# A graph layer kernel: thinned neighbours marked by indirect writes of single elements instead of by matmuls, and PSUM banks shared out anew

## The chip, the cores and the metric

The kernel runs on one core of one Trainium2 chip. The metric is device microseconds of one execution, start to end. The times of the kernel before are 1410.16, 1417.88 and 1423.46 us; their median is 1417.88 us.

## The reference, cut to what matters

There are 16 batches of 1024 nodes with 64 channels. Layer 0 is a normalised adjacency product; layer 1 thins the neighbour lists, takes quantiles over the sorted neighbour values in every channel, and ends with two small matmuls.

```python
neigh = (adj_ > 0) & ~eye
rank = jnp.cumsum(ni, axis=-1) - ni
nb = ni.sum(-1)
skip = jnp.where(nb > T, (nb + K - 1) // K, 1)          # T = 10, K = 2
rem = neigh & (sk > 1) & (rank % sk == sk - 1) & mask[:, :, None]
rem = rem | jnp.swapaxes(rem, 1, 2)
adj_d = jnp.where(rem, 0.0, adj_)
vals = jnp.where(nd[..., None], x[:, None, :, :], jnp.inf)
s = jnp.sort(vals, axis=2)                               # quantiles 0.25, 0.5, 0.75
h = jax.nn.relu(out @ W1 + b1)
y = h @ W2 + b2
```

So a node with more than 10 neighbours marks at most two of them, the one at rank skip-1 and the one at rank 2*skip-1, and each marked edge goes in both directions.

## The kernel before, in words

Two batches make a group `g`; there are 8 groups. Each batch is first prepared, and then the two batches of a group are worked on together.

Preparation of a batch: SP loads the adjacency in 8 pieces of 512 KB into `AT` (ring of 3). DVE makes 0/1 neighbours from them (`neighbors`, L1163), PE multiplies them with the features (`messages`, L557) and takes running counts over them (`ranks_up`, L568) into one of the three banks of `psT`; ACT brings the counts into `VR` (`ranked`, L841). `VR` holds one row of codes, features, neighbour count and mask for every node, and there is a single `VR`: the counts of the next batch wait until its rows have been scattered. Then the thinned edges are found and taken out for the whole 1024 x 1024 matrix: POOL computes ranks from the neighbour counts (`thin`, L1439 to L1456, 11 small instructions for each half of a batch), ACT writes the distance of each code to them (`distance`, L848), DVE turns that into a matrix of removals `RM` (`removed`, L1169), PE adds code, removal and transposed removal (`codes`, L589 to L596) in `psT`, ACT brings the result back through a Relu (`coded`, L867) and counts what is left (`valid`, L873). POOL sorts nodes into classes by their number of neighbours (`classes`, from L1465; `nodes_ahead` on PE, `ahead` on ACT, `place` on DVE, whose result `RS` POOL turns into `IDX` at L1480), and scatters the eight tiles of rows to HBM in that order with one indirect DMA each (`scatter`, L1505).

Work on a group: SP reads the sorted rows back in 128-row pieces (`RR`, two buffers, L530), PE transposes them (`positions_up`, L604), ACT stores the positions (L884). DVE makes one-hot matrices from them (`one_hots`, L1194, L1205, L1209), PE gathers neighbour features with these (`gather`, L651, L660) into two banks `psG`, ACT brings them out (L952, L957). DVE sorts: L1276 and L1277 for the 128 nodes with most neighbours, the hub, L1227 and L1232 for the others. Weights are applied (L1243, L1252), and `overflow` ends the sorting of a group with the memset of `MARK` (L1370). Then come the two small matmuls and, on POOL, the indirect writes of the output (`put`, L1546).

The order of the work of all engines is one string, `ORDER`: each letter stands for one step of a strand, and each engine takes its own part of each step in that order. SP's loads are in the same order, so a load that waits holds up the loads behind it. POOL, too, takes its instructions strictly in order. In the string, U is a load of adjacency, D a count, s a code tile, c a count of what is left, S a scatter, L a load of sorted rows, d a half of a one-hot chunk, and B and r the steps of thinning.

## Time and profile before

| what | us |
|---|---|
| median of three runs | 1417.88 |
| span of the profiled execution, first to last instruction | 1381.6 |
| median less span, what lies around it | 36.3 |
| TensorE (PE) busy | 1209.3 |
| VectorE (DVE) busy | 1129.0 |
| ScalarE (ACT) busy | 958.9 |
| GpSimd (POOL) busy | 734.6 |

The profile is of one execution. A busy time is the time in which an engine has an instruction running; a matmul's end is modelled, so PE's figure is an upper reading. The wait rows give the idle time of an engine just before an instruction and the engine whose work ended it. A stretch between two times can be asked for its own busy times, and that tells more than a mean over the whole span.

### The profile page before, as it was taken

Reading aid. Unit: us, or ns where it says so; the run is one execution under the profiler, and the core shown is the slowest. Engines: PE = TensorE matmul, PEld = TensorE weight load, DVE = VectorE, ACT = ScalarE, POOL = GpSimd, SP = SyncE. Lnnn points to the kernel's source line nnn. Section 1 sums busy time; section 2 is a strip of 40 time slices with the busy share of each in tenths; the row PEclk is TensorE's granted clock in tenths of the full one; section 3 lists DMA queues with packets and bytes.
Section 4 is the critical chain, followed back from the end, with each engine's and each line's share of the span. In section 5 each row is a group of like instructions: output and inputs, shape, how many; then the busy total and the mean of one; then the engine's idle time right before and its main releaser. Section 6 shows DMA issues by size and latency. Waiting matters only on the chain.

```text
span 1381.6 us, 32444 instructions
## 1 busy us (share of the span) xinstructions
PE 1209.3 (88%) x12833; PEld 893.1 (65%) x12833; DVE 1129.0 (82%) x2060; ACT 958.9 (69%) x1755; POOL 734.6 (53%) x988
## 2 busy tenths in 40 slices
PE   4979999999899989999999989899898999688543
PEld 4757776867577676667767667667666676555221
DVE  3441379989899889999799989889897999888980
ACT  1787778887789678888678677777775888743311
POOL 0463434454558753876547665774477553721325
PEclk9988799999999999999799998999898999889655
DMA  4355543554245433535444433446134341331000
GB/s 136 130 161 181 157 140 107 196 176 145 83 156 159 141 113 102 159 115 171 126 135 138 135 109 112 140 136 208 52 116 125 103 141 46 133 87 36 8 9 15
DMA packets 119032, 167.08 MB, mean 121 GB/s; under 512 B 58816, under 2 KB 59472, under 8 KB 118864
## 3 DMA queue, kind: packets, MB, share of 16 engines
q1 hardware_dynamic: 103168, 117.72, 28.9%
q0 software_dynamic: 14336, 46.42, 8.8%
q8 instruction: 101, 1.65, 0.5%
q10 hardware_dynamic: 1360, 0.74, 0.2%
q14 instruction: 67, 0.55, 0.1%
HBM read 114.25 MB, written 50.59 MB: 119 GB/s over the span
## 4 chain that ended last, share of the span: by engine, by line
PE 42%; DVE 23%; POOL 14%; issue 8%; ACT 7%; DMA 4%; ACTq 1%; SPq 0%; POOLq 0%; DVEq 0%
PE psL L557 11%; PE psG L660 6%; PE psT L568 5%; POOL out L1546 5%; PE psG L651 4%; DVE HUB L1276 4%; DVE HUB L1277 4%; PE psM L706 3%; DVE OHB L1209 3%; PE psT L589 2%; POOL rows L1505 2%; PE psT L593 2%; PE psT L604 2%; PE psT L596 2%; DVE OHB L1194 2%
## 5 line engine op out<-in xcount | busy, mean ns | idle before, releaser
L557 PE MATMUL psL<-H0A,AT 128*128 128x65 f32 x2048 | 274.3, 296 | 12.4 <-issue 8.6
L557 PEld LDWEIGHTS psL<-H0A,AT 128*128 128x128 f32 x2048 | 266.3, 212 | 24.3 <-issue 21.1
L1505 POOL DMA_INDIRECT rows<-VR,IDX x128 | 171.1, 1336 | 87.3 <-ACT JUNK L873 48.0
L1276 DVE TENSOR_TENSOR HUB<-HUB 128x1472 f32<-128x1472 f32 (+6 forms) x224 | 184.8, 825 | 11.9 <-ACT HUB L984 9.0
L1277 DVE TENSOR_TENSOR HUB<-HUB 128x1472 f32<-128x1472 f32 (+6 forms) x224 | 188.6, 842 | 0.0
L568 PE MATMUL psT<-UM,NEIT 128*128 128x512 f16 (+3 forms) x1024 | 161.0, 306 | 21.0 <-ACT VR L841 11.3
L867 ACT ACTIVATE VR<-psT 128x512 f16<-128x512 f32 x256 | 149.1, 598 | 43.4 <-PE psT L596 33.3
L660 PE MATMUL psG<-OHB,HL 128*64 128x384 f16 (+5 forms) x2048 | 170.2, 316 | 9.3 <-DVE OHB L1209 4.2
L1546 POOL DMA_INDIRECT out<-FR x128 | 154.5, 1207 | 38.4 <-issue 36.3
L651 PE MATMUL psG<-OHB,HL 128*64 128x256 f16 (+1 forms) x2560 | 152.9, 279 | 6.9 <-ACT HUB L952 3.7
L848 ACT ACTIVATE RM<-VR,SK 128x1024 f16<-128x1024 f16 x128 | 138.0, 1151 | 20.2 <-POOL SK L1456 20.2
L651 PEld LDWEIGHTS psG<-OHB,HL 128*64 128x64 f16 x2560 | 137.0, 116 | 19.9 <-DVE OHB L1194 8.9
L568 PEld LDWEIGHTS psT<-UM,NEIT 128*128 128x128 f16 x1024 | 88.8, 101 | 88.6 <-ACT VR L841 15.0
L660 PEld LDWEIGHTS psG<-OHB,HL 128*64 128x64 f16 x2048 | 106.7, 111 | 58.9 <-issue 9.1
L984 ACT ACTIVATE HUB<-HUB 128x1472 f32<-128x1472 f32 (+5 forms) x168 | 90.7, 540 | 69.5 <-DVE HUB L1277 67.8
L873 ACT ACTIVATE JUNK<-VR 128x1024 int8<-128x1024 f16 x128 | 134.4, 1058 | 0.1
L1163 DVE TENSOR_SCALAR NEIT<-AT 128x1024 f16<-128x1024 f32 x128 | 90.8, 730 | 30.7 <-DMA AT<-in_adjt 30.7
L593 PEld LDWEIGHTS psT<-CH,RM 128*128 128x128 f16 x1024 | 83.7, 100 | 48.9 <-issue 4.6
L841 ACT ACTIVATE VR<-psT,CF 128x512 f16<-128x512 f32 x128 | 80.7, 697 | 46.9 <-PE psT L568 41.9
L589 PE MATMUL psT<-VR,CH 128*128 128x512 f16 x256 | 100.6, 393 | 10.3 <-DVE RM L1169 6.2
L593 PE MATMUL psT<-CH,RM 128*128 128x128 f16 x1024 | 107.3, 223 | 0.0
L841 ACT ACTIVATE VR<-psT,CB 128x512 f16<-128x512 f32 x128 | 79.7, 692 | 32.7 <-POOL CB L1426 16.7
(135 smaller groups left out, 2273.0 us busy)
## 6 DMA issues: line engine op xcount, KB each, us to landing
AT<-in_adjt SPq DMA_DIRECT2D x128, 512.0 KB, 4.7
RR<-rows SPq DMA_DIRECT2D x128, 288.0 KB
FR<-rows SPq DMA_DIRECT2D x16, 272.0 KB, 4.7
X<-in_x SPq DMA_DIRECT2D x16, 256.0 KB, 3.7
h<-VR SPq DMA_DIRECT2D x16, 256.0 KB
rows<-VR,IDX POOLq DMA_INDIRECT x128, 4.3
out<-FR POOLq DMA_INDIRECT x128
CH<-in_ch ACTq DMA_DIRECT2D x1, 192.0 KB, 4.5
```

Source lines behind the costliest of these rows:

```text
L557: m = e.matmul(ps["L"][:, 65 * t:65 * t + 65], AT[:, n % RING, kk, t * P:t * P + P], H0A[:, T * b + 2 * kp + kk, :], start=(kp == kk == t ...
L568: m = e.matmul(o[:, kk * P:COLS], half(t // 4)[:, at:at + P], UM[:, 0:COLS - kk * P], start=(kk == 0), stop=(kk == 3), skip_group_check=True)
L593: e.matmul(oj, RM[:, t, k * P:k * P + P], idh, start=False, stop=False, skip_group_check=True)
L651: m = e.matmul(bk[C * b:C * b + C, at:at + cols], HL[:, part, (2 * g + b) % 3, k, :], OHB[:, n % 2, b, k * cols:k * cols + cols], start=(k ...
L660: m = e.matmul(bk[C * b:C * b + C, 0:cols], HL[:, part, (2 * g + b) % 3, k, :], OHB[:, n % 2, b, kk * cols:kk * cols + cols], start=(k == ...
L841: e.activation(VR[:, t, COLS * ch:COLS * ch + COLS], t_bank(u), ACT.Identity, bias=bias).then_inc(t_empty, 1)
L848: e.activation(RM[:, t, :], VR[:, t, 0:N], ACT.Abs, bias=SK[:, 3, t:t + 1]).then_inc(a_abs, 1)
L867: e.activation(VR[:, k, 512 * ch:512 * ch + 512], t_bank(u), ACT.Relu).then_inc(t_empty, 1)
L1276: e.tensor_tensor(b0, a0, a1, ALU.max)
L1277: e.tensor_tensor(b1, a0, a1, ALU.min).then_inc(v_bat, 1)
L1505: e.indirect_dma_start(row_d[:, :], bass.IndirectOffsetOnAxis(ap=IDX[:, gb % 2, t:t + 1], axis=0), VR[:, t, :].bitcast(I32), None).then_in ...
L1546: e.indirect_dma_start(out_d, bass.IndirectOffsetOnAxis(ap=dst, axis=0), fr[:, rt, 0:2 * C].bitcast(F32), None).then_inc(d_out[g % 2], 16)
```

## The change

The matrix of removals is gone, with `codes`, `coded`, `distance` and `removed`. Codes stay in `VR` as they are, without Relu, and are scattered at once; the features, counts and flags go with them. What is thinned is taken out in HBM afterwards, for the hub's 128 rows alone, in five new steps for each batch: `hub` (SP loads the first 128 rows into `HB`), `thin` (8 small instructions on POOL), `find` (one `max_index` on DVE, which looks for the two marked ranks in each of the 128 rows), `rank` (`targets`: 9 small instructions on POOL, two indirect reads of 128 single elements from a table of ranks that SP writes in step `key`, and two indirect writes of 128 single fp16 elements into the nodes' own rows), and `take` (`take_out`: 5 small instructions and two indirect writes of 128 single elements into the rows of the other nodes). What is written is `GONE`, the value -1. The loads of sorted rows now wait for the last two writes (`d_gone`) instead of the scatters. The count of what is left runs on ACT over the loaded row `RR`, before its buffer is given back, instead of over `VR`. Batches have HBM tensors of their own for their rows, and a row is 2580 bytes in place of 2576. `psT` has two banks in place of three, and the gather three in place of two. Two broadcast matmuls are added to each `flags` step, which report if more than 128 nodes have over 10 neighbours; the branch for such inputs is rewritten too, and it is entered only if a flag is set. `ORDER` is a new string: it differs all through.

```diff
-TB = 3
+TB = 2
+GB = 3
...
-            add("T", "thin", g, b, hf)
-            for t in range(4 * hf, 4 * hf + 4):
-                add("B", "abs", g, b, t)
-                add("r", "rem", g, b, t)
...
-            for ch in range(2):
-                add("s", "sc", g, b, k, ch)
-            add("c", "cn", g, b, k)
             add("S", "sca", g, b, k)
+        for c, kind in (("H", "hub"), ("T", "thin"), ("i", "find"), ("B", "rank"), ("r", "take")):
+            add(c, kind, g, b)
...
+                add("c", "cn", g, b, rt)
...
-        ps = {k: ctx.enter_context(nc.psum_tensor("ps" + k, [P, 512], F32)) for k in ("L", "S", "G0", "G1", "M")}
+        ps = {k: ctx.enter_context(nc.psum_tensor("ps" + k, [P, 512], F32)) for k in ("L", "S", "G0", "G1", "G2", "M")}
...
+                elif kind == "key":
+                    g, b = a
+                    gb = 2 * g + b
+                    w.wait_ge(o_idx, gb + 1)
+                    e.dma_start(rank_d[gb].rearrange("(t p) o -> p (t o)", p=P), IDX[:, gb % 2, :], allow_slow_non_contiguous=True).then_inc(d_rt, 16)
+                elif kind == "hub":
+                    g, b = a
+                    gb = 2 * g + b
+                    for t in range(T):
+                        w.wait_ge(d_sca[t], 16 * (gb + 1))
+                    if gb:
+                        w.wait_ge(v_find, gb)
+                        w.wait_ge(o_adr, gb)
+                    e.dma_start(HB[:, :].bitcast(I32), rows(g, b)[0:P, :]).then_inc(d_hub, 16)
                 elif kind == "ldr":
                     g, b, rt = a
                     n = nth["ldr", g, b, rt]
-                    for t in range(T):
-                        w.wait_ge(d_sca[t], 16 * (2 * g + b + 1))
+                    w.wait_ge(d_gone[b], 32 * (g + 1))
                     if n >= 2:
                         w.wait_ge(t_full, t_use("turn", filled[n - 2][0], filled[n - 2][2]) + 1)
-                    n0 = (2 * g + b) * N + rt * P
-                    e.dma_start(RR[:, n % 2].bitcast(I32), row_d[n0:n0 + P, 0:R_X1 // 2]).then_inc(d_row[n % 2], 16)
+                        w.wait_ge(a_cn, n - 1)
+                    e.dma_start(RR[:, n % 2].bitcast(I32), rows(g, b)[rt * P:rt * P + P, 0:R_X1 // 2]).then_inc(d_row[n % 2], 16)
...
-            def codes(g, b, k, ch):
-                w.wait_ge(v_rem, T * (2 * g + b + 1))
-                o = t_free("sc", g, b, k, ch)
-                e.matmul(o, idh, VR[:, k, 512 * ch:512 * ch + 512], start=True, stop=False, skip_group_check=True)
-                for j in range(4):
-                    t = 4 * ch + j
-                    oj = o[:, j * P:j * P + P]
-                    e.matmul(oj, RM[:, t, k * P:k * P + P], idh, start=False, stop=False, skip_group_check=True)
-                    if t == k:
-                        e.matmul(oj, CH[:, CH_4K, :], idh, start=False, stop=False, skip_group_check=True)
-                e.matmul(o, idh, RM[:, k, 512 * ch:512 * ch + 512], start=False, stop=True,
-                         skip_group_check=True).then_inc(t_full, 1)
...
+                for b in range(2):
+                    m = e.matmul(o[0:32, :], FLO[:, b:b + 1].to_broadcast([P, 32]),
+                                 UM[:, P:P + 1].to_broadcast([P, COLS]), start=False, stop=(b == 1), skip_group_check=True)
...
-                if half == 0 and u >= 2:
-                    w.wait_ge(g_empty, u - 1)
+                if half == 0 and u >= GB:
+                    w.wait_ge(g_empty, u + 1 - GB)
...
-            def distance(g, b, t):
-                gb = 2 * g + b - 1
-                if gb >= 0:
-                    w.wait_ge(t_full, t_use("sc", gb // 2, gb % 2, T - 1, 1) + 1)
-                w.wait_ge(o_thin, 2 * (2 * g + b) + t // 4 + 1)
-                e.activation(RM[:, t, :], VR[:, t, 0:N], ACT.Abs, bias=SK[:, 3, t:t + 1]).then_inc(a_abs, 1)
...
-            def coded(g, b, k, ch):
-                u = t_use("sc", g, b, k, ch)
-                w.wait_ge(t_full, u + 1)
-                e.activation(VR[:, k, 512 * ch:512 * ch + 512], t_bank(u), ACT.Relu).then_inc(t_empty, 1)
-
-            def valid(g, b, k):
-                w.wait_ge(t_empty, t_use("sc", g, b, k, 1) + 1)
-                if nth["cn", g, b, k] >= 2:
-                    w.wait_ge(a_cn, nth["cn", g, b, k] - 1)
-                e.activation(JUNK[:, k % 2, :], VR[:, k, 0:N], ACT.Sign,
-                             accum_out=feat(VR, R_NV)[:, k, :]).then_inc(a_cn, 1)
+            def valid(g, b, rt):
+                n = nth["cn", g, b, rt]
+                w.wait_ge(d_row[n % 2], 16 * (n // 2 + 1))
+                if g:
+                    w.wait_ge(t_full, t_use("nvt", g - 1) + 1)
+                if n >= 2:
+                    w.wait_ge(a_cn, n - 1)
+                e.activation(JUNK[:, n % 2, :], RR[:, n % 2, 0:N], ACT.Sign,
+                             accum_out=NV[:, T * b + rt:T * b + rt + 1]).then_inc(a_cn, 1)
...
-            def removed(g, b, t):
-                rm = RM[:, t, :]
-                w.wait_ge(a_abs, nth["abs", g, b, t] + 1)
-                e.tensor_scalar(rm, rm, SK[:, 4, t:t + 1], -4096.0, ALU.is_equal, ALU.mult).then_inc(v_rem, 1)
+            def find(g, b):
+                gb = 2 * g + b
+                w.wait_ge(d_hub, 16 * (gb + 1))
+                w.wait_ge(o_thin, gb + 1)
+                if gb:
+                    w.wait_ge(o_ji, gb)
+                e.max_index(FOUND[:, :], NW[:, :], HB[:, 0:N]).then_inc(v_find, 1)
...
+            def thin(g, b):
                 gb = 2 * g + b
+                nb, mk = (HB[:, at:at + 2].bitcast(F32) for at in (R_NB, R_MK))
+                on, mid, both = HSK[:, 0:1], HSK[:, 1:2], HSK[:, 2:4]
+                w.wait_ge(d_hub, 16 * (gb + 1))
                 if gb:
+                    w.wait_ge(v_find, gb)
+                e.tensor_scalar(mid, nb, 0.5, 0.25, ALU.mult, ALU.add).then_inc(o_in, own.up())
+                e.tensor_scalar(on, nb, 10.0, None, ALU.is_gt).then_inc(o_in, own.up())
+                w.wait_ge(o_in, own.n)
+                e.tensor_scalar(mid, mid, 8388608.0, None, ALU.add).then_inc(o_in, own.up())
+                e.tensor_tensor(on, on, mk, ALU.mult).then_inc(o_in, own.up())
+                w.wait_ge(o_in, own.n)
+                e.tensor_scalar(both[:, 0:1], mid, -8388608.0, None, ALU.add).then_inc(o_in, own.up())
+                e.tensor_scalar(both[:, 1:2], mid, -8388608.0, 2.0, ALU.add, ALU.mult).then_inc(o_in, own.up())
+                w.wait_ge(o_in, own.n)
+                e.tensor_copy(NW[:, 0:2], both).then_inc(o_thin, 1)
+                e.tensor_scalar(HSK[:, 4:6], both, nb, on, ALU.is_le, ALU.mult).then_inc(o_in, own.up())
+
+            def flat(gb):
+
+                return row_d[gb][:, :].rearrange("n (f o) -> (n f) o", o=1)
+
+            def targets(g, b):
+                gb = 2 * g + b
+                there = HSK[:, 4:6]
+                w.wait_ge(v_find, gb + 1)
+                w.wait_ge(o_in, own.n)
+                e.tensor_copy(AT2[:, 0:2], FOUND[:, 0:2]).then_inc(o_in, own.up())
+                w.wait_ge(o_in, own.n)
+                e.tensor_tensor(AT2[:, 0:2], AT2[:, 0:2], there, ALU.mult).then_inc(o_in, own.up())
+                w.wait_ge(o_in, own.n)
+                e.tensor_copy(JI[:, :], AT2[:, 0:2]).then_inc(o_ji, 1)
+                e.tensor_tensor(HSK[:, 6:8], there, CF[:, CF_SKIP:CF_SKIP + 2], ALU.mult).then_inc(o_in, own.up())
+                e.tensor_tensor(BACK[:, :], there, CF[:, CF_BACK:CF_BACK + 2], ALU.mult).then_inc(o_in, own.up())
+                w.wait_ge(o_ji, gb + 1)
+                w.wait_ge(d_rt, 16 * (gb + 1))
+                for q in range(2):
+                    e.indirect_dma_start(RK[:, q:q + 1], None, rank_d[gb][:, :],
+                                         bass.IndirectOffsetOnAxis(ap=JI[:, q:q + 1], axis=0)).then_inc(d_rk, 16)
+                w.wait_ge(o_in, own.n)
+                e.tensor_tensor(AT2[:, 0:2], AT2[:, 0:2], HSK[:, 6:8], ALU.add).then_inc(o_in, own.up())
+                e.tensor_tensor(BACK[:, :], BACK[:, :], CF[:, CF_DUMP:CF_DUMP + 2], ALU.add).then_inc(o_in, own.up())
+                w.wait_ge(o_in, own.n)
+                e.tensor_tensor(AT2[:, 0:2], AT2[:, 0:2], CF[:, CF_DUMP:CF_DUMP + 2], ALU.add).then_inc(o_in, own.up())
+                w.wait_ge(o_in, own.n)
+                e.tensor_copy(ADR[:, 0:2], AT2[:, 0:2]).then_inc(o_in, own.up())
+                w.wait_ge(o_in, own.n)
+                for q in range(2):
+                    e.indirect_dma_start(flat(gb), bass.IndirectOffsetOnAxis(ap=ADR[:, q:q + 1], axis=0),
+                                         GONE[:, :], None).then_inc(d_own, 16)
+
+            def take_out(g, b):
+                gb = 2 * g + b
+                there = HSK[:, 4:6]
+                node = HB[:, R_ND:R_ND + 2].bitcast(F32)
+                at = AT2[:, 2:4]
+                w.wait_ge(o_in, own.n)
+                w.wait_ge(d_rk, 32 * (gb + 1))
+                e.tensor_copy(at, RK[:, :]).then_inc(o_in, own.up())
+                w.wait_ge(o_in, own.n)
+                e.tensor_scalar(at, at, float(ROW), node, ALU.mult, ALU.add).then_inc(o_in, own.up())
+                w.wait_ge(o_in, own.n)
+                e.tensor_tensor(at, at, there, ALU.mult).then_inc(o_in, own.up())
+                w.wait_ge(o_in, own.n)
+                e.tensor_tensor(at, at, BACK[:, :], ALU.add).then_inc(o_in, own.up())
+                w.wait_ge(o_in, own.n)
+                e.tensor_copy(ADR[:, 2:4], at).then_inc(o_adr, 1)
+                w.wait_ge(o_adr, gb + 1)
+                w.wait_ge(d_own, 32 * (gb + 1))
+                for q in range(2):
+                    e.indirect_dma_start(flat(gb), bass.IndirectOffsetOnAxis(ap=ADR[:, 2 + q:3 + q], axis=0),
+                                         GONE[:, :], None).then_inc(d_gone[b], 16)
...
-                w.wait_ge(a_cn, nth["cn", g, b, t] + 1)
```

Two places show what the order does. The first is POOL during the scatters of batch 1, the second batch of the first group. Before, from `IDX` on (SK, GE, IN belong to the classes, NEIT to the neighbours, CB to the counts):

```order
L1480 TENSOR_SCALAR IDX<-RS 128x8
L1418 TENSOR_TENSOR NEIT<-NEIT,CH 128x4x128
L1505 DMA rows<-VR,IDX 16384x644 x4
L1488 TENSOR_TENSOR VR<-X,XC 128x4x64
L1505 DMA rows<-VR,IDX 16384x644 x4
L1424 TENSOR_SCALAR CB<-VR 128x4
L1426 TENSOR_TENSOR CB<-CB,VR 128x4
L1418 TENSOR_TENSOR NEIT<-NEIT,CH 128x4x128
```

In the changed kernel, where six of the eight scatters of batch 1 have been issued (HSK, AT2, BACK and ADR hold what `targets` and `take_out` compute; rows0 is batch 0's tensor, rows1 batch 1's):

```order
L1513 CAST AT2<-FOUND 128x2
L1515 TENSOR_TENSOR AT2<-AT2,HSK 128x2
L1517 CAST JI<-AT2 128x2
L1518 TENSOR_TENSOR HSK<-HSK,CF 128x2
L1519 TENSOR_TENSOR BACK<-HSK,CF 128x2
L1523 DMA RK<-ranks0,JI 128x1 x2
L1526 TENSOR_TENSOR AT2<-AT2,HSK 128x2
L1527 TENSOR_TENSOR BACK<-BACK,CF 128x2
L1529 TENSOR_TENSOR AT2<-AT2,CF 128x2
L1531 CAST ADR<-AT2 128x2
L1534 DMA rows0<-GONE,ADR 1320960x1 x2
L1614 DMA rows1<-VR,IDX 1024x645 x2
```

The eight scatters of batch 1 are no longer issued four and four: six go first, then stand two reads and two writes of single elements of batch 0, and the last two scatters behind them.

The second place is DVE ahead of the first one-hots (OHB), with the removals (RM) before:

```order
L1169 TENSOR_SCALAR RM<-RM,SK 128x1024 x4
L1163 TENSOR_SCALAR NEIT<-AT 128x1024
L1169 TENSOR_SCALAR RM<-RM,SK 128x1024 x4
L1178 TENSOR_TENSOR PLACE<-AHEAD,IN 128x128
L1180 TENSOR_REDUCE RS<-PLACE 128x8
L1163 TENSOR_SCALAR NEIT<-AT 128x1024
L1140 SCALAR_TENSOR_TENSOR HL<-VR,HL 128x512
L1205 TENSOR_SCALAR OHB<-POSA 128x2x1536 x2
```

and in the changed kernel, with the normalisation of batch 2 (ST, VR) ahead of them:

```order
L1192 TENSOR_SCALAR NEIT<-AT 128x1024 x2
L1123 TENSOR_REDUCE ST<-VR 128x8
L1126 TENSOR_SCALAR ST<-ST 128x8
L1134 TENSOR_REDUCE ST<-VR 128x8
L1192 TENSOR_SCALAR NEIT<-AT 128x1024 x2
L1138 RECIPROCAL ST<-ST 128x8
L1140 SCALAR_TENSOR_TENSOR VR<-XC,ST 128x8x64
L1210 TENSOR_TENSOR PLACE<-AHEAD,IN 128x128
L1212 TENSOR_REDUCE RS<-PLACE 128x8
L1237 TENSOR_SCALAR OHB<-POSA 128x2x1536 x5
```

The eight passes L1169 of batch 2 have gone from here, the normalisation of batch 2 has moved ahead of the first one-hots, and five one-hot pieces stand in a row where two did. Of the loads of adjacency, 27 stand ahead of the first one-hot step in the string before and 31 in the new one; of the counts it is 54 in both.

## Rows read from the trace of the kernel before

**Rows 1.** Busy times and the TensorE clock in 40 slices, from the page.

```profile
PE 1209.3 (88%) x12833; PEld 893.1 (65%) x12833; DVE 1129.0 (82%) x2060; ACT 958.9 (69%) x1755; POOL 734.6 (53%) x988
PEclk9988799999999999999799998999898999889655
```

**Rows 2.** Stretches: length, PE, PEld, DVE, ACT, POOL, clock, DMA share, GB/s.

```profile
0.00:163.00 163.00, 130.95 (x954) 107.31 (x955) 53.02 (x103) 103.21 (x162) 62.48 (x135) 0.87 0.49 152
163.00:1200.00 1037.00, 967.75 (x10739) 718.02 (x10736) 944.83 (x1706) 800.03 (x1469) 613.81 (x793) 0.96 0.41 131
1200.00:1348.50 148.50, 99.26 (x1122) 64.21 (x1120) 129.80 (x251) 51.76 (x118) 40.44 (x44) 0.75 0.14 41
1348.50:1381.60 33.10, 11.31 (x24) 3.59 (x24) 1.40 (x3) 3.91 (x6) 17.92 (x18) 0.50 0.05 16
163.00:1348.50 1185.50, 1067.01 (x11858) 782.23 (x11854) 1074.63 (x1956) 851.78 (x1587) 654.25 (x836) 0.93 0.38 120
```

**Rows 3.** DVE's waits, 163 to 1348.5 us: total, times, longest.

```profile
DVE W L1252 <- PE psS L693: 16.7, 15, 5.3
DVE OHB L1205 <- PE psG L660: 11.2, 12, 4.6
DVE OHB L1209 <- PE psG L651: 6.2, 4, 3.3
DVE OHB L1194 <- PE psG L660: 4.1, 4, 1.9
DVE RM L1169 <- ACT RM L848: 3.8, 6, 1.6
DVE RM L1169 <- issue: 2.7, 1, 2.7
```

**Rows 4.** Groups of instructions that the change takes out.

```profile
L589 PE MATMUL psT<-VR,CH 128*128 128x512 f16 x256 | 100.6, 393 | 10.3 <-DVE RM L1169 6.2 <-ACT VR L867 2.9 <-ACT AHEAD L855 0.9
L593 PE MATMUL psT<-CH,RM 128*128 128x128 f16 x1024 | 107.3, 223 | 0.0
L595 PE MATMUL psT<-CH 128*128 128x128 f16 x128 | 28.7, 224 | 0.0
L596 PE MATMUL psT<-RM,CH 128*128 128x512 f16 x256 | 99.4, 388 | 0.0
L867 ACT ACTIVATE VR<-psT 128x512 f16<-128x512 f32 x256 | 149.1, 598 | 43.4 <-PE psT L596 33.3
L848 ACT ACTIVATE RM<-VR,SK 128x1024 f16<-128x1024 f16 x128 | 138.0, 1151 | 20.2 <-POOL SK L1456 20.2
L1169 DVE TENSOR_SCALAR RM<-RM,SK 128x1024 f16<-128x1024 f16 x128 | 64.8, 556 | 11.0 <-ACT RM L848 8.3 <-issue 2.7
```

**Rows 5.** Groups: one DVE pass over 1024 elements; POOL's indirect DMAs.

```profile
L1105 DVE TENSOR_REDUCE ST<-H0A 128x16 f32<-128x1024 f32 x8 | 9.7, 1213 | 1.4 <-ACT H0A L827 1.4
L1505 POOL DMA_INDIRECT rows<-VR,IDX x128 | 171.1, 1336 | 87.3 <-ACT JUNK L873 48.0 <-issue 27.8 <-DVE VR L1111 10.6
L1546 POOL DMA_INDIRECT out<-FR x128 | 154.5, 1207 | 38.4 <-issue 36.3 <-POOL FR L1538 1.6 <-POOL IDX L1480 0.4
```

**Rows 6.** Instructions on tile SK: length, then DVE, ACT, POOL busy.

```profile
0.00:1381.60 1381.60, 64.80 (x128) 138.03 (x128) 171.69 (x416) 0.92 0.39 121
```

**Rows 7.** Scatter L1505's landing; the hardware queue's packets, MB, share.

```profile
DMA to landing us min/median/max: 2.9/4.3/8.3
q1 hardware_dynamic: 103168, 117.72, 28.9%
```

**Rows 8.** Timeline of POOL, batch 1: start, length, what, idle before.

```profile
115.03 0.61 POOL L1480 TENSOR_SCALAR IDX<-RS 128x8 int32<-128x8 f32 x1 [14.03 <-DVE RS L1180]
117.04 1.09 POOL L1505 DMA_INDIRECT rows<-VR,IDX  x1 [0.15 <-issue]
130.26 0.96 POOL L1505 DMA_INDIRECT rows<-VR,IDX  x1 [0.30 <-issue]
```

**Rows 9.** Timeline of DVE at the first one-hots.

```profile
162.98 1.85 DVE L1205 TENSOR_SCALAR OHB<-POSA 128x3072 f16<-128x3072 f16 x2
```

283 lines of the change are left out of this document (170 added, 113 removed).

## Prediction

> **What bounds the kernel now.** I read the page's busy times first [rows 1]: PE is busy for 88% of the span and DVE for 82%, so no single engine explains the time. The stretches say more [rows 2]. Up to the first one-hots at 163.0 us [rows 9] DVE has work for only 53.0 us: two batches have to be prepared before anything can be sorted, and PE is busy for 131. From 163 to 1200 us PE stands at 967.8 of 1037 (93%) and DVE at 944.8 (91%): both are nearly full, and each waits for the other in turn. From 1200 to 1348.5 us the preparation is over, PE falls to 99.3 of 148.5 and DVE carries the stretch with 129.8. The last 33.1 us, after the last group's `MARK`, are the small matmuls and the output. So between the first one-hots and the last `MARK` DVE does 1074.6 us of work in 1185.5 and idles for 110.9. The reader is to see there that a PE relieved of a quarter of its work does not give that quarter back: DVE's own work is the floor. The third view is what DVE waited for [rows 3]: four rows that end in PE make 16.7 + 11.2 + 6.2 + 4.1 = 38.2 us, and two before the removals, which go altogether, 3.8 + 2.7 = 6.5 us.
>
> **What goes.** PE loses 100.6 + 107.3 + 28.7 + 99.4 = 336.0 us, ACT 149.1 + 138.0 = 287.1 us and DVE 64.8 us [rows 4]. PE comes to 1209.3 - 336.0 = 873.3, ACT to 958.9 - 287.1 = 671.8 [rows 1]. Of PE's part nothing but its share in DVE's waits reaches the end; ACT's is hidden, as ACT was never full (851.8 of 1185.5) [rows 2]. The two broadcast matmuls of a flag step, 32 in all, priced like L596's 388 ns [rows 4], are 12.4 us on a PE with room; without that cover they would cost that.
>
> **What comes on DVE.** 16 `max_index` over 1024 codes. No row shows the instruction. The nearest is a pass of DVE over 1024 elements at one element a step, 1213 ns [rows 5]: 16 x 1.21 = 19.4 us, which I take. The ends are 556 ns, the fp16 pass L1169 [rows 4] (8.9 us), and two such passes of 1213 ns (38.8 us). DVE then has 1129.0 - 64.8 + 19.4 = 1083.6 us of work.
>
> **What comes on POOL.** `thin` was 11 instructions for each half batch, 352 of the 416 that touch SK. Now a batch has 2 left in `classes`, and 8, 9 and 5 in the new steps: 24 x 16 = 384. At 171.69 / 416 = 0.41 us each [rows 6] that is 32 more, 13 us. The indirect DMAs are 6 x 16 = 96. POOL's own price for one is 1207 to 1336 ns [rows 5] for 128 descriptors, and these have 128 too: 96 x 1.27 = 122 us. POOL comes to 734.6 + 13 + 122 = 870 us, some two thirds of the new span. That stays hidden as long as the order puts these steps well ahead of the loads. If a descriptor of one element costs POOL half of that, it is 61 us, if it costs double, 244 us, and POOL would be at 992 us, still under DVE.
>
> **What comes on the queues.** The rank table is 1024 elements of 4 bytes for a batch, the indirect DMAs add 768 and the hub load 128: 1920 x 16 = 30,720 packets. The hardware queue's 103,168 packets took 28.9% of 16 engines' span [rows 7], 62 ns each; 30,720 of these are 119 us on one of them shared by all 16, that is 7.4 us of time for the whole kernel's DMA. Against a DMA share of 0.41 [rows 2] that is hidden. Were each new packet twice as dear, it would be 15 us, hidden as well. SP's queue gets two new waiting places for a batch: the hub load (for eight scatters) and the loads of sorted rows (for `d_gone`). What stands behind them is the adjacency for later batches, for which DVE's neighbours and PE's messages wait. I take it as covered, since four batches are loaded ahead, and price it in the second rival.
>
> The Trainium skill, "DMA: Bandwidth & Descriptors", section Specifications, says that a transfer under 512 bytes makes the DMA engine read, change and write back. No row here has packets of 2 bytes. If by that rule each of the three landings of single elements took twice the 4.3 us that I use below, the chain before the first one-hots would be 12.9 us longer, and the forecast 1339 in place of 1326.
>
> **The banks.** Two banks of `psT` make PE wait for ACT's reading sooner; PE, at 873 of 1290 us, has the time. The third gather bank lets PE begin the next chunk while ACT still reads the last, and helps against part of the 11.2 + 6.2 + 4.1 us [rows 3]. I count both within the idle time below, at 0, with ends of -10 and +10 us.
>
> **The start.** The first one-hots wait for batch 1 to be in HBM. POOL makes batch 1's `IDX` at 115.0 us after waiting 14.0 for DVE, which in turn waited behind the code tiles of PE and ACT; its eight scatters go from 117.0 to 131.2, 1.27 us each if nothing held them, so 10.2 instead of 14.2 [rows 8]. In the changed kernel codes no longer stand before `IDX`: 115.0 - 14.0 + 3 for the class matmuls = 104, and batch 0's scatters, which were held in the same way, give back about 6: 98. Then follow eight scatters (10, so 108), landing 4.3 [rows 7] (112), the hub load, priced the same (117), find, five small instructions and two reads (1.2 + 2.0 + 2.5: 123), landing (127), five small ones, two writes and landing (2.0 + 2.5 + 4.3: 136). Before, 27.5 us lay between the last landing of batch 1 (131.2 + 4.3 = 135.5) and the first one-hots. I let them be 12, since PE no longer has two batches of codes in arrears: 148 us. The bounds are 130, if PE and the loads run at their best, and 163, as before. So the chain of the new round trips costs nearly all that the codes give back here: 15 us are won. DVE will have done 53.0 - 24 x 0.556 (L1169) + 2 x 1.2 (find) + 4 us (two more pieces of neighbours and the norm of batch 2) = 46.1 us by then.
>
> **The sum.** From 148 us to the last `MARK` DVE has 1083.6 - 46.1 - 1.4 (after `MARK` [rows 2]) = 1036.1 us of work. Its idle time was 110.9; less 38.2 for PE and 6.5 for the removals it is 66.2, and I add 6 for new waits (finds that stand before their hub row has landed, one-hots after a late load): 72, with ends of 30 and 111. Span = 148 + 1036.1 + 72 + 33.1 = 1289 us. The execution profiled had a span of 1381.6 and the median of the runs is 1417.9, 36.3 above it. I take the same distance: 1289 + 36.3 = 1325.5, so **1326 us**, 6.5% less.
>
> **Rivals.** *DVE's idle time stays.* DVE's waits are the shape of the order, not PE's load: first one-hots at 163, idle 110.9 - 6.5 = 104.4. Span 163 + 1036.1 + 104.4 + 33.1 = 1336.6, time 1373. For it: only a third of the idle time is put down to PE [rows 3]. Against it: PE is at 93% where those waits arise [rows 2]. 17%.
>
> *The chain of round trips is exposed.* This is the slower side. From a batch's last scatter landing to its last single write landing are 136 - 112 = 24 us that were not there. Where a group's loads catch up with its preparation, SP stands at `d_gone`, the adjacency behind it waits, and DVE has neither positions nor neighbours. Before the first one-hots this is counted. Afterwards the kernel is slower from 1432 us on: (1432 - 1326) / 24 = 4.4 of the 14 remaining batches exposed in full; half of the 16, 8, would give 1326 + 8 x 24 = 1518. Against it: the batches are prepared nearly two groups ahead, 31 loads stand before the first one-hot step. 5%.
>
> *TensorE's clock.* The granted clock is 0.96 of 2.4 GHz from 163 to 1200 us, and 0.75 from 1200 on, where PE is busy for 67%; at the end it is 0.50, so 1.2 GHz [rows 2]. After the change PE has gaps everywhere, as it has now from 1200 on. If DVE then gets the share it has there, 129.8 / 148.5 = 87.4%, its 1036.1 us take 1185.5; span 148 + 1185.5 + 33.1 = 1366.6, time 1403. 11%. The Trainium skill, "TensorE: Matmul & The Clock Gate", section "HAM oscillation — how this bites in real kernels", says that bursts of matmuls with waits between them keep falling back to half rate and start there again. The trace agrees in that its low slices lie at the start and the end, where PE waits [rows 1]; it does not say what that costs DVE.
>
> *Better than forecast.* With one-hots at 130 and 30 us idle: 130 + 1036.1 + 30 + 33.1 = 1229, time 1265.5. 10%. *The change does not do what it says*, as when a flag is set or PE's relief buys nothing: 1418, 2%.
>
> **How the numbers follow.** The forecast has 55%. The range goes from 1270 to 1400: from near the better case to near the clock case, it holds the first rival and leaves about 2 in 10 outside. A measurement of this kernel can tell about 1% from no change. All but the slower case, the last and a tail of the clock case lie more than 14 us below 1417.9: faster 0.92, within 1% 0.04, slower 0.04.
>
> **What would show it.** First one-hots near 148 us; DVE busy near 1084 and near 90% or more from there to the last `MARK`; PE busy near 890 with rows of DVE waiting for psS and psG shrunk to a half or less; `max_index` near 1.2 us; the 96 indirect DMAs near 1.27 us. I am wrong if the loads of RR wait on the single writes in the middle of the run, if POOL passes 80% busy, or if the clock from 163 to 1200 us falls under 0.85 and DVE's waits for PE grow.

## The result, and the profile after

The changed kernel takes 1532.7 us, the median of 4 runs (1529.3 to 1542.4). The kernel before, run beside it on the same chip, takes 1420.2 us. The ratio is 1.083, 95% interval 1.076 to 1.090: 8.3% slower, where 6.5% faster was forecast.

The page of the profile after, span, busy times and clock:

```profile
span 1528.0 us, 29035 instructions
PE 1163.8 (76%) x11201; PEld 828.0 (54%) x11201; DVE 1089.3 (71%) x1964; ACT 701.6 (46%) x1371; POOL 814.3 (53%) x1120
PEclk9867898888887887889988797989989898669755
```

Every engine is less busy, by share, than before, except POOL. DVE's work is what the forecast said (1083.6), ACT's nearly so (671.8), and the time is longer all the same. The stretches of the kernel after answer to those of [rows 2]: up to the first one-hots, from there to the last `MARK`, and the tail.

```profile
0.00:169.00 169.00, 117.31 (x758) 96.14 (x759) 47.86 (x89) 53.32 (x87) 74.29 (x139) 0.80 0.61 161
169.00:1495.00 1326.00, 1035.06 (x10420) 728.24 (x10418) 1040.01 (x1873) 644.34 (x1279) 722.05 (x963) 0.84 0.40 109
1495.00:1528.00 33.00, 11.41 (x24) 3.59 (x24) 1.38 (x2) 3.91 (x6) 17.93 (x18) 0.50 0.05 17
```

DVE has 1040.0 us of work in the middle stretch (forecast 1036.1) but takes 1326.0 for it: it idles for 286.0 us, where 110.9 stood before and 72 in the forecast. The span is 239 us longer than forecast, and this idle time makes 214 of it and a start at 169.0 in place of 148 another 21. One caution on such differences between the two traces: the execution traced before had a span of 1381.6 us, 37 less than the 1418 or so of the runs beside which the change was timed, so up to that much of a difference may lie between executions and not between kernels. What DVE waited for in that stretch (total, times, longest), against [rows 3]:

```profile
DVE W L1284 <- PE psS L711: 37.2, 17, 8.9
DVE HUB L1308 <- ACT HUB L992: 27.0, 19, 7.4
DVE OHB L1241 <- PE psG L678: 20.3, 8, 7.2
DVE W L1259 <- issue: 17.9, 2, 9.1
...
DVE ANY L1450 <- ACT ROWS L927: 10.9, 1, 10.9
```

The wait for psS has doubled (16.7 to 37.2), and each row shown holds at least one single wait of 7 to 11 us, where the longest of [rows 3] is 5.3. So the reader should look at what stands behind single long holes, and not only at the engines' loads. The queues after, against [rows 7], and the new instructions by group:

```profile
q1 hardware_dynamic: 122112, 123.07, 30.4%
...
L1201 DVE FIND_INDEX8 FOUND<-NW,HB 128x8 uint32<-128x1024 f16 x16 | 19.5, 1217 | 0.0
L1201 DVE MATCH_VALUE_LOAD FOUND<-NW,HB 128x8 f16 x16 | 1.4, 86 | 17.4 <-POOL NW L1501 8.8 <-issue 8.6
...
L1523 POOL DMA_INDIRECT RK<-ranks,JI x32 | 40.3, 1258 | 8.7 <-issue 8.7
...
L1556 POOL DMA_INDIRECT rows<-GONE,ADR x32 | 39.5, 1234 | 19.0 <-DMA rows<-GONE,ADR 7.3 <-issue 6.5 <-POOL ADR L1552 5.2
L1534 POOL DMA_INDIRECT rows<-GONE,ADR x32 | 37.3, 1165 | 10.2 <-issue 5.2 <-POOL ADR L1531 5.0
```

Each new piece costs its own engine what the forecast gave it: 1217 ns for the find, 1165 to 1258 ns for an indirect DMA. The loss is in what they do to others, as the experiments show.

**Where one hole comes from.** A timeline of the kernel after around the table write of one batch: start, length, what, and in brackets the idle time before.

```profile
1013.38 0.40 SPq L541 DMA_DIRECT2D ranks<-IDX  x1
1013.87 1.56 SPq L520 DMA_DIRECT2D AT<-in_adjt  x3
1014.21 1.74 POOL L1614 DMA_INDIRECT rows<-VR,IDX  x1 [0.86 <-DVE VR L1140]
...
1030.40 0.69 ACT L857 ACTIVATE VR<-psT,CF 128x512 f16<-128x512 f32 x1 [11.31 <-DMA rows<-VR,IDX]
1031.14 1.25 PE L596 MATMUL psT<-UM,NEIT 128*128 128x512 f16 x4 [11.73 <-ACT VR L857]
1031.68 0.15 DVE L1450 TENSOR_TENSOR ANY<-ANYS 1x1 f32<-1x1 f32 x1 [10.89 <-ACT ROWS L927]
1033.64 0.72 POOL L1598 TENSOR_TENSOR VR<-X,XC 128x256 f32<-128x256 f32 x1 [12.76 <-DVE XC L1183]
```

The rank table (4 KB) is sent at 1013.38. A scatter issued at 1014.21 and the ones behind it land so late that ACT stands for 11.31 us, and PE, DVE and POOL after it. The stretches of the same place show what the DMA does meanwhile (length, PE, PEld, DVE, ACT, POOL, clock, DMA share, GB/s):

```profile
1013.00:1016.00 3.00, 3.00 (x28) 1.80 (x26) 2.85 (x6) 0.88 (x2) 1.94 (x2) 0.50 0.16 1
1016.00:1024.00 8.00, 3.41 (x60) 2.19 (x56) 4.59 (x8) 0.73 (x2) 4.01 (x3) 0.93 0.84 20
1024.00:1030.00 6.00, 0.00 (x0) 0.00 (x0) 0.00 (x0) 0.00 (x0) 0.00 (x0) 0.50 0.95 341
```

For some 10 us after the write 1 and then 20 GB/s move, though adjacency and scatters are queued and the DMA engines count as 84% busy; then the backlog goes at 341. The table's own 1024 packets of 4 bytes don't fill this time: by the packet records they all start between 1014.3 and 1015.0 us and last at most 9 ns each. There are 16 such writes. In the packet records 222 packets last over 2 us, in 16 groups, each within 11 us after a table write; in the trace before there is one such packet.

### The profile page after: what moved, and what is told of

It reads as the page before. It is cut to its first block and busy times, and to the rows that moved or that the text cites. A ratio compares the mean times of both kernels' runs of the same rounds, so it can differ in the third digit from the quotient of the medians.

```text
span 1528.0 us, 29035 instructions
## 1 busy us (share of the span) xinstructions
PE 1163.8 (76%) x11201; PEld 828.0 (54%) x11201; DVE 1089.3 (71%) x1964; ACT 701.6 (46%) x1371; POOL 814.3 (53%) x1120
## 5 line engine op out<-in xcount | busy, mean ns | idle before, releaser
L596 PE MATMUL psT<-UM,NEIT 128*128 128x512 f16 (+3 forms) x1024 | 195.3, 330 | 60.8 <-ACT VR L857 32.7
L678 PE MATMUL psG<-OHB,HL 128*64 128x384 f16 (+5 forms) x2048 | 201.0, 347 | 15.7 <-DVE OHB L1237 9.5
L669 PE MATMUL psG<-OHB,HL 128*64 128x256 f16 (+1 forms) x2560 | 175.1, 295 | 38.3 <-DVE OHB L1226 21.0
L1614 POOL DMA_INDIRECT rows<-VR,IDX x128 | 148.6, 1161 | 50.6 <-issue 35.0
L880 ACT ACTIVATE JUNK<-RR 128x1024 int8<-128x1024 f16 x128 | 135.0, 1055 | 24.8 <-DMA RR<-rows 24.8
L619 PE MATMUL psT<-CH,RR 128*128 128x128 f16 x1024 | 88.9, 237 | 33.5 <-DMA RR<-rows 13.7
L1237 DVE TENSOR_SCALAR OHB<-POSA 128x3072 f16<-128x3072 f16 (+5 forms) x128 | 88.8, 718 | 33.7 <-PE psG L678 11.6
L891 ACT ACTIVATE POSA<-psT 128x1024 f16<-128x1024 f16 x80 | 81.0, 1020 | 60.7 <-PE psT L619 57.2
L711 PE MATMUL psS<-COEF,CH 128*64 128x24 f16 (+5 forms) x1280 | 57.6, 221 | 62.9 <-POOL COEF L1643 35.4
L619 PEld LDWEIGHTS psT<-CH,RR 128*128 128x128 f16 x1024 | 68.7, 107 | 58.7 <-issue 39.3
```

The costliest lines, as they stand in the source:

```text
L596: m = e.matmul(o[:, kk * P:COLS], half(t // 4)[:, at:at + P], UM[:, 0:COLS - kk * P], start=(kk == 0), stop=(kk == 3), skip_group_check=True)
L619: m = e.transpose(o[:, k * P:k * P + P], RR[:, n % 2, k * P:k * P + P], idh)
L669: m = e.matmul(bk[C * b:C * b + C, at:at + cols], HL[:, part, (2 * g + b) % 3, k, :], OHB[:, n % 2, b, k * cols:k * cols + cols], start=(k ...
L678: m = e.matmul(bk[C * b:C * b + C, 0:cols], HL[:, part, (2 * g + b) % 3, k, :], OHB[:, n % 2, b, kk * cols:kk * cols + cols], start=(k == ...
L880: e.activation(JUNK[:, n % 2, :], RR[:, n % 2, 0:N], ACT.Sign, accum_out=NV[:, T * b + rt:T * b + rt + 1]).then_inc(a_cn, 1)
L1614: e.indirect_dma_start(rows(g, b), bass.IndirectOffsetOnAxis(ap=IDX[:, gb % 2, t:t + 1], axis=0), VR[:, t, :].bitcast(I32), None).then_inc ...
```

## The experiments

Eighteen kernels. Theory A: the element-wise table write chokes the DMA. Theory B: the new mechanism's chain, split later into held loads (B1), POOL (B2) and the finds (B3). Theory C and D: banks and order. The kernels were run in six sets (e1 to e4, e5 to e7, e8 and e9, e10 to e12, e13 to e16, e17 and e18), each on one chip beside the kernel before, and a ratio is to that; round brackets give its 95% interval. The kernel before took 1373.9 to 1444.6 us over the sets, so absolute times are compared inside one set only. Most ratios came out alike when a kernel was run again (the change 1.083 and 1.082, e8 and e15 1.036 and 1.038, e5 and e16 0.965 and 0.968), but e1 and e14, one kernel too, gave 1.021 and 1.047. So the parts were measured once more together.

### The table write: e1, e2, e3

e1 (the layout of the table changes, from 1024 runs of 4 bytes to 128 runs of 32, so POOL works out the address, 8 j - 1023 floor(j / 128), with five instructions more; the branch for overflowing inputs, which isn't entered, keeps the old one):

```diff
-                    e.dma_start(rank_d[gb].rearrange("(t p) o -> p (t o)", p=P), IDX[:, gb % 2, :], allow_slow_non_contiguous=True).then_inc(d_rt, 16)
+                    e.dma_start(rank_d[gb].rearrange("(p t) o -> p (t o)", p=P), IDX[:, gb % 2, :]).then_inc(d_rt, 16)
...
```

> The changed kernel (1532.7 us), but SP writes each rank table in 128 runs of 32 bytes instead of 1024 single elements of 4 bytes, and POOL works out the address in that layout with 5 more small instructions for each batch. Theory A, the element-wise table write chokes all DMA: in the changed kernel's trace the stretch 1016 to 1024 us, just after one such write, has a DMA share of 0.84 and moves only 20 GB/s, and there are 16 such writes. Without them 6 to 10 us are won for each where nothing covers it: 1532.7 - 16 x 8 = about 1405 us (1370 to 1440), and no stretch behind a table write with a high DMA share at a few tens of GB/s. Theory B, the new round trips and what SP holds behind them (hub load, loads of sorted rows waiting for the single writes): these are all still here, so 1505 to 1535 us. Theory C, the order and the shared banks: also 1505 to 1535 us.

e2 and e3 add the table write to the kernel before, in step `key` of SP's queue. e2 writes it by elements; e3 has the `(p t)` layout of e1 in its place:

```diff
+                    w.wait_ge(o_idx, gb + 1)
+                    e.dma_start(rank_d[gb].rearrange("(t p) o -> p (t o)", p=P), IDX[:, gb % 2, :], allow_slow_non_contiguous=True).then_inc(d_rt, 16)
```

> The kernel before (1420.2 us) and one thing more: SP writes each batch's rank table of 1024 elements, 4 bytes each, element by element, as the changed kernel does, at the same letter of the order. Nobody reads it. Theory A (the table write chokes all DMA for 3 to 10 us): 16 x 3 to 16 x 10, so 1470 to 1580 us, with DVE's and ACT's waits for DMA grown. Theories B and C (round trips; order and banks): 16,384 packets of 62 ns shared by 16 queues are 4 us, hidden, so 1410 to 1430 us.

> As the last, but the table goes in 128 runs of 32 bytes: the same wait of SP for IDX, the same 4 KB, an eighth of the packets. Theory A: within 1% of the kernel before, 1410 to 1435 us, so that the loss of the last is down to the single elements and not to SP's wait. Rival (SP's queue, held for IDX at this place): the same loss as the last.

Measured on one chip: before 1444.6; e1 1478.1 (1.021, 1.015 to 1.028); e2 1521.2 (1.054, 1.045 to 1.063); e3 1455.3 (1.005, 1.0005 to 1.010). So 4 KB a batch that nobody reads cost the kernel before 66 us more by elements than in runs, 4.1 us each. Packets over 2 us: 186 in e2, none in e1 and e3. Theory A holds: e2 lies in its range, and e3 within its 1% of the kernel before (the absolute 1410 to 1435 us are missed, as all of this set runs longer). e1 is the miss: 1478 where A had 1370 to 1440. It is still slower than the kernel before, so A is not the whole.

Stretches of 8 us behind two table writes of the kernel after (sent at 840.2 and 1203.0), and behind two of e14, which is e1 once more:

```profile
842.00:850.00 8.00, 6.00 (x56) 3.85 (x54) 6.67 (x14) 0.00 (x0) 4.02 (x4) 0.93 0.30 15
...
1205.00:1213.00 8.00, 3.09 (x30) 1.50 (x26) 5.55 (x17) 0.00 (x0) 6.03 (x7) 0.91 0.75 24
```

```profile
796.50:804.50 8.00, 6.54 (x56) 3.87 (x54) 7.15 (x14) 0.00 (x0) 5.28 (x4) 0.88 0.99 307
...
1140.00:1148.00 8.00, 4.29 (x34) 2.12 (x34) 6.07 (x18) 1.72 (x4) 6.17 (x7) 0.91 0.91 307
```

These are clear cases; not every write does as much. Taken in the same way behind all 16 writes, from 1.8 to 9.8 us after each is issued, the core's DMA moves 15 to 131 GB/s in the kernel after, with a median of 50, and 70 to 335 with a median of 250 in e14. In the old order it is 11 to 85, median 24, in e2, and 63 to 346, median 147, in e3.

### The banks: e4

The kernel before with `TB = 2` and three gather banks, and the waits that go with them.

> The kernel before with the banks of the changed one alone: two for counts and positions in place of three, three for the gather in place of two, in the old order, with its codes still going through them. Theory A: 0 to +2%, 1420 to 1450 us, for the codes press on these banks here and no longer do after the change. Theory C (the banks carry the loss): 1490 us or more.

Measured: 1536.9 us, 1.060 (1.052 to 1.068). That is Theory C's number: in the old order these banks cost 92 us. Which of the two, the third bank of `psT` lost or the one of the gather gained, does it was not tried apart. Whether they cost that in the changed kernel too is the next question.

### What the relief is worth: e5, e6, e7

e5 drops `hub`, `thin`, `find`, `rank`, `take` and the table from the changed kernel; e6 drops `codes`, `coded`, `distance` and `removed` from the kernel before; e7 is e6 with the banks of e4. In e6 and e7 the 4096 that `codes` adds at each node's own place goes too, and POOL's old `thin`, the 352 small instructions that fed the removals, stays. In e5 the loads wait as before the change:

```diff
-                    w.wait_ge(d_gone[b], 32 * (g + 1))
+                    for t in range(T):
+                        w.wait_ge(d_sca[t], 16 * (2 * g + b + 1))
```

> The changed kernel with all that is new for thinning left out: no rank table, no hub load, no thin, find, rank and take, and the loads of sorted rows wait for the scatters again. Nothing is thinned, so this leaves out part of the computation. Its order (less those letters) and its banks stay. Theory B (what is left of the loss after the table write, 1478 against the 1326 forecast, is the chain of round trips, POOL's 96 indirect DMAs and the 16 finds): 1340 to 1380 us. Theory D (it is the new order and the banks): 1440 us or more.

> The kernel before with its removals left out: no code tiles on PE, no distance and no Relu on ACT, no removal on DVE. Nothing is thinned, so this leaves out part of the computation. The old order (less those letters) and the old banks stay. It tells what taking 336 us off PE, 287 off ACT and 65 off DVE is worth where nothing else changes. If DVE's own work is the floor, as forecast: 1290 to 1340 us. If the relief buys little, because the order's waits stay: 1390 to 1430 us. With the last run it gives the price of order and banks: Theory D wants at least 80 us between the two, Theory B under 30.

> The last kernel with the banks of the changed one: two for counts and positions, three for the gather. With the codes still there these banks cost 6% (1537 against 1445). If that was the codes' pressing on psT: within 2% of the last run. If counts and positions alone need the third bank: 4 to 6% over it, and then the forecast's 0 for the banks is wrong by 60 to 80 us.

Measured on one chip: before 1424.7; e5 1369.9 (0.965); e6 1369.8 (0.965); e7 1431.5 (1.011, 1.002 to 1.021). Three things follow. With all work for removals gone and nothing in its place, the kernel gains 55 us, between the two numbers expected of e6. The new order with the new banks takes as long as the old order with the old banks, so Theories C and D fall as explanations of the loss: what the banks cost in the old order, 4.5% (e7 over e6), is made good in e5. Whether the new order does that alone is not shown, for e5 also has less on POOL (594.3 us busy against 724.3 in e6). And the mechanism of thinning makes the rest of the loss, as Theory B has it. The stretch between first one-hots and last `MARK` of e6:

```profile
154.40:1337.00 1182.60, 954.01 (x10412) 705.71 (x10412) 1030.83 (x1853) 622.57 (x1259) 644.50 (x837) 0.88 0.37 120
```

PE's work is down, and DVE idles for 1182.6 - 1030.8 = 151.8 us, more than the 110.9 before. The granted clock is 0.88 where it was 0.93.

### Held loads or POOL: e8, e9

e8 sends the single writes to a side tensor and lets the loads wait for the scatters, on top of e1; e9 drops `rank` and `take` too.

> The changed kernel with the table in 128 runs (1.021 of the kernel before), and one thing undone: the single writes go to a side tensor of the same shape, and the loads of sorted rows wait for the scatters, so nothing waits for these writes. All work is still issued, but nothing is thinned, so this leaves out part of the computation. Without the whole mechanism the ratio was 0.965, with it 1.021: 0.056, some 80 us. Theory B1 (the loads, held at the end of the chain of round trips, carry it): ratio 0.97 to 0.985. Theory B2 (POOL's extra time, 860.5 us busy against 594.3, which in its strict order delays its other steps: PE waited 41.8 us for POOL's COEF additions against 14.7): ratio 1.01 to 1.02, hardly better.

> As the last, and POOL's steps rank and take are left out too: 96 indirect DMAs and some 300 small instructions less on POOL. Table, hub load, thin and find stay, so DVE's 16 finds with their waits (20.9 + 27.3 us) are still there. Nothing is thinned, so this leaves out part of the computation. Theory B2 (POOL): ratio 0.97 to 0.98, at least 0.03 under the last run. Theory B3 (DVE's finds and what they wait for): 1.00 to 1.01, and the last run no lower. Theory B1: the same as the last run, 0.97 to 0.985.

Measured on one chip: before 1437.2; e8 1487.3 (1.036, 1.028 to 1.044); e9 1401.9 (0.974, 0.968 to 0.980). The two POOL steps cost 85 us when nobody waits for their writes. The four runs of e8 lie between 1465.1 and 1501.8 us; by the two shorter ones the step is 72 us. B1 and B3 fall as main causes. B2 has e9 right, but its 1.01 to 1.02 for e8 is missed as well.

### Less on POOL: e10, e11, e12

e10 lets DVE add up `COEF` in place of POOL (e1 otherwise); e11 writes POOL's arithmetic with 128 instructions fewer, for instance

```diff
-                e.tensor_scalar(mid, nb, 0.5, 0.25, ALU.mult, ALU.add).then_inc(o_in, own.up())
...
-                e.tensor_scalar(mid, mid, 8388608.0, None, ALU.add).then_inc(o_in, own.up())
+                e.tensor_scalar(mid, nb, 0.5004, 8388608.0, ALU.mult, ALU.add).then_inc(o_in, own.up())
```

and e12 does both.

> The changed kernel with the table in 128 runs (ratio 1.021), and the two additions of COEF for each group made by DVE in place of POOL, at the same letter of the order. This takes the one wait away in which PE is seen to wait for POOL's arrears (41.8 us in all, L1653), and 18 us from POOL; DVE gets some 6 us. Theory B2 (POOL is late in its strict order and hands that on): ratio 1.00 to 1.01 and PE's wait before psS under 10 us. Rival (the arrears come out elsewhere, or DVE now waits for ACT at that place): 1.015 to 1.03.

> The changed kernel with the table in 128 runs, with POOL's arithmetic written shorter: thin, rank and take have 5, 10 and 4 small instructions for each batch in place of 8, 14 and 5, so 128 fewer; the same table reads and single writes at the same addresses. At about 0.45 us each, 58 us of the 266 us by which POOL's busy time exceeds that without the mechanism (860.5 against 594.3). Theory B2, in proportion to the 0.056 that the mechanism costs: 0.012 less, so a ratio of 1.00 to 1.015. If only the indirect DMAs or their landings count: 1.02, as before.

> Both edits together. If each takes its part off the same arrears: 0.99 to 1.00, no more than a tie with the kernel before, and some 8 to 9% under the changed kernel as it stands.

Measured on one chip: before 1373.9; e10 1428.6 (1.040), e11 1433.3 (1.043), e12 1408.0 (1.023, 1.015 to 1.030). All three are above what was expected, which started from e1's 1.021; the same kernel stood at 1.047 when it was run again (e14). What holds inside the set: moving `COEF` to DVE takes 25 us off e11, though it gives DVE more to do. PE's wait before psS for `COEF` was 41.4 us in e11, and in e12, where it is DVE's addition that PE waits for, 9.8. Whether either edit alone gains anything over e1 is not shown, since e1 was not in this set. e12 is the best version that computes the same, and it is still slower than the kernel before.

### The parts on one chip: e13 to e16

The changed kernel, e1, e8 and e5 once more.

> The changed kernel as it stands, on one chip with the next three. 1.083 of the kernel before, as measured; chips differ (the kernel before took 1374 to 1445 us on four), so only differences within this call are read.

> The changed kernel with the rank table in 128 runs, once more. Theory A: 60 to 110 us under e13, by the element-wise table write alone.

> As e14, with the single writes into a side tensor and the loads of sorted rows waiting for the scatters alone (nothing is thinned, so this leaves out part of the computation). Theory B1 (held loads): at least 30 us under e14. Theory B2 (POOL): within 15 us of e14.

> The changed kernel without table, hub load, thin, find, rank and take (nothing is thinned, so this leaves out part of the computation). Theory B2: 70 to 110 us under e15. Against the kernel before it gives what the relief is worth with the new order and banks: 0.96 to 0.97.

| kernel | us | ratio, interval | step |
|---|---|---|---|
| before | 1379.1 | | |
| e16, no thinning | 1338.4 | 0.968 (0.960 to 0.976) | -40.7 relief, order and banks |
| e15, thinning, loads not held | 1427.2 | 1.038 (1.028 to 1.049) | +88.8 mechanism |
| e14, loads held | 1445.6 | 1.047 (1.038 to 1.056) | +18.4 held loads |
| e13, table by elements | 1493.2 | 1.082 (1.074 to 1.090) | +47.5 table write |

The held loads are the one step whose intervals overlap; e8 against e1, of two different sets, had pointed the other way. Its 18.4 us lie between what B1 wanted (30 at least) and what B2 did (15 at most); it is small, and may be nothing. The table write fell short of the 60 us that was expected at least. The mechanism's 88.8 us hold the table in runs, the hub load, `thin` and find as well as `rank` and `take`.

### POOL's time or single elements on the DMA: e17, e18

e17 keeps the small instructions of `rank` and `take` and drops their indirect DMAs; e18 keeps the DMAs with fixed addresses and drops the arithmetic. Both on top of e15.

> The kernel with the table in runs and loads not held (1.038 of the kernel before on the last chip, 1.036 on an earlier one), without the 96 indirect DMAs of rank and take; the 19 small instructions for each batch stay (nothing is thinned, so this leaves out part of the computation). Without both the ratio was 0.974. Theory P (POOL's time, whatever fills it): of 193.6 us of POOL's busy time in these steps (847.4 less 653.8) the DMAs have 111 and the rest 82, so the arithmetic alone costs about 0.4 of the 0.062: 1.00 (0.99 to 1.01). Theory Q (the traffic and landings of single elements): 0.97 to 0.98.

> The counterpart: the 96 indirect DMAs stay, with fixed addresses worked out once, and the 19 small instructions for each batch go (nothing is thinned, so this leaves out part of the computation). Theory P: about 0.6 of the 0.062: 1.01 (1.00 to 1.02). Theory Q: 1.03 to 1.04, the whole loss.

Measured: 1.000 (0.997 to 1.003) and 0.995 (0.992 to 0.999). Theory Q wanted 1.03 to 1.04 for the DMAs alone, and falls: small reads and writes by indirect DMA don't choke anything here, and no packet of e18 lasts over 2 us. Theory P has e17 right and e18 too high (1.00 to 1.02 expected). Against e9's 0.974 the arithmetic alone makes 0.026 and the DMAs alone 0.021; with both, e8 has 0.062, 0.015 more than the sum. If some of either fits into POOL's slack, and not both, this is what one would see. But the numbers come from different sets, and one kernel's ratio moved by 0.026 between sets (e1, e14), so that they don't add up is not shown.

Three stretches from first one-hots to last `MARK`, of e16, e15 and e14, show the loss on DVE, which has 1016.6, 1029.2 and 1028.0 us of work in them and idles for 123.4, 201.4 and 225.8:

```profile
166.60:1306.60 1140.00, 971.37 (x10420) 696.15 (x10418) 1016.57 (x1845) 640.61 (x1279) 537.40 (x571) 0.90 0.39 123
```

```profile
162.20:1392.80 1230.60, 991.26 (x10420) 706.42 (x10418) 1029.16 (x1873) 642.51 (x1279) 775.76 (x1033) 0.88 0.37 117
```

```profile
160.90:1414.70 1253.80, 985.56 (x10420) 702.17 (x10418) 1028.03 (x1873) 642.03 (x1279) 770.93 (x1033) 0.88 0.37 115
```

POOL goes from 537 to 776 us, 63% of that stretch, which nobody would call full. Two places show how its arrears, the steps that it does late because others stand before them, reach the other engines. One is PE's wait before psS for `COEF`, in e16 and in e14.

```profile
PE psS L704 <- POOL COEF L1635: 14.8, 4, 10.4
```

```profile
PE psS L712 <- POOL COEF L1653: 53.8, 5, 17.0
```

The other is DVE's find, which needs `NW` from POOL's `thin`. POOL first, then DVE, in e14:

```profile
1066.81 0.98 POOL L1566 DMA_INDIRECT rows<-GONE,ADR  x1 [0.31 <-issue]
1067.82 1.27 POOL L1658 TENSOR_TENSOR FR<-FR,Z 128x512 f32<-128x512 f32 x1
1069.06 0.20 POOL L1493 TENSOR_SCALAR HSK<-HB 128x1 f32<-128x1 f32 x1
...
1070.52 0.18 POOL L1502 CAST NW<-HSK 128x2 f16<-128x2 f32 x1
```

```profile
1070.79 0.09 DVE L1202 MATCH_VALUE_LOAD FOUND<-NW,HB 128x8 f16 x1 [9.54 <-issue]
1070.87 1.22 DVE L1202 FIND_INDEX8 FOUND<-NW,HB 128x8 uint32<-128x1024 f16 x1
```

POOL never rests from 1062.5 on: scatter, `take` with its two writes, an addition, and only then `thin`. DVE stands for 9.54 us, for want of seven small instructions that take 1.6 us from first to last.

## Why the prediction was wrong, step by step

**Queues (forecast: 7.4 us, hidden).** The step that failed worst in kind. It priced the table's 16,384 elements, and 14,336 others, by the mean time of a packet, 62 ns shared by 16. There is a slip in that sum: 30,720 times 62 ns are 1905 us on one engine and 119 us shared by 16; the forecast took the 119 us for one engine's and divided by 16 once more. (The same slip makes the 4 us in what was expected of e2.) Done right, its price for the table alone is 16,384 x 62 ns / 16 = 63 us, near what was measured, but only by luck, and at a DMA share of 0.41 it would still have been called hidden. By their own records the 4-byte packets last only 7 to 9 ns each, some 8 us in all shared by 16; what they cost is that what is queued behind them moves little for some 8 to 10 us. Worth 47.5 us on one chip, and 66 us in e2 against e3. A sum of packet times can't show this; the layout `(t p) o` in the diff, with its leave for non-contiguous elements, was the sign. The Trainium skill, "DMA: Bandwidth & Descriptors", section "🎯 Rules for kernel authors", says that a non-contiguous last dim becomes one descriptor per element and should be rearranged to be contiguous. e3 against e2 agrees and gives it a price. The Trainium skill's rule on transfers under 512 bytes (same page, section "Specifications"), which the prediction weighed, doesn't tell the two apart: runs of 32 bytes are under it as well and cost 0.5%. The 12,288 single elements of the indirect DMAs were not the load that was forecast either: the packet records show them as 1536 packets of 16 or 32 bytes.

**POOL (forecast: hidden below DVE's load).** The total was even too high (870 against 814.3), but the conclusion "hidden" was wrong by 85 us for `rank` and `take` (e9 against e8), 89 us with hub load, `thin` and find (e15 against e16). The total came out lower because a scatter took 1161 ns where it had taken 1336 [rows 5]. What failed is the condition that the forecast set, that POOL had to pass 80% busy to hurt; it hurt at 53%. POOL takes its instructions strictly in order, so a step of 10 us is 10 us for whatever stands behind it. Its price of 0.41 us for a small instruction is a mean over two kinds of neighbourhood, as other rows of e14's POOL show:

```profile
1063.57 0.20 POOL L1554 CAST AT<-RK 128x2 f32<-128x2 int32 x1
1063.88 0.26 POOL L1556 TENSOR_SCALAR AT<-AT,HB 128x2 f32<-128x2 f32 x1
...
1072.60 0.76 POOL L1516 TENSOR_TENSOR AT<-AT,HSK 128x2 f32<-128x2 f32 x1
1074.28 1.10 POOL L1519 TENSOR_SCALAR TQ<-AT 128x2 f32<-128x2 f32 x1
1075.46 1.51 POOL L1521 TENSOR_SCALAR TQ<-TQ 128x2 f32<-128x2 f32 x1
```

**The idle time (forecast: 110.9 less 38.2 less 6.5).** With PE relieved, DVE's waits for PE were to go. e6 takes the load away and puts nothing in its place, and DVE's idle time rose to 151.8; its waits for psS and psG together were 40.9 us, against 42.5 in the trace before. So the 38.2 us were no measure of what relief would bring. Why is open between two readings. One is the first rival's: these waits are the latency of a step in the order, not PE's load. The other is the clock rival's: PE, with gaps, gets a lower clock, so each of its steps is longer. e6 has 0.88 for 0.93, and DVE is busy for 87.2% of its stretch, where that rival, from the 87.4% of the tail, had said the same. No run holds the clock while it takes the work away. Relief was worth 55 us in e6, and 41 in e16 with order, banks and POOL's lighter load counted in, where the forecast, without its 25 us for finds and new waits, gave it 117.

**PE (forecast: 873 us busy).** Measured 1163.8. The groups of the line view overlap: PE's matmul groups before sum to 1433 us against 1209.3 on the page, so 336.0 could not be taken off it whole. e6, which takes off just these, has 1080.3. The clock, 0.84 in place of 0.93 in the middle stretch, goes with it, but how much of the difference it makes was not taken apart. The clock rival was right that the level would fall, but it isn't what makes the change slower than the kernel before: e6 and e16 are faster than that at 0.88 and 0.90. The sign that was set for it, under 0.85 from 163 to 1200 us, did not come; it is 0.86 there, though DVE's waits for psS and psG did grow, to 92.8 us from first one-hots to last `MARK`.

**DVE, find, indirect DMAs.** Right: 1040.0 us of work for 1036.1, 1217 + 86 ns for 1.21 us, 1165 to 1258 ns for 1.27 us.

**The start (forecast: 148 us).** Measured 169.0. Rows of the kernel after for batch 1, on POOL and DVE:

```profile
96.55 0.19 POOL L1590 CAST IDX<-RS 128x8 int32<-128x8 f32 x1
...
114.23 0.97 POOL L1614 DMA_INDIRECT rows<-VR,IDX  x1 [0.30 <-issue]
...
146.91 0.98 POOL L1556 DMA_INDIRECT rows<-GONE,ADR  x1 [0.30 <-issue]
```

```profile
169.01 1.83 DVE L1237 TENSOR_SCALAR OHB<-POSA 128x3072 f16<-128x3072 f16 x2 [10.89 <-ACT Z L899]
```

`IDX` came as forecast (98), the last scatter 7 us late, and the last single write was issued 11 us after the time at which it was to have landed. But e16, with no chain, starts at 166.6, and e14, with it, at 160.9. So the chain doesn't set this start, and counting it step by step was beside the point. In the old order e6 starts at 154.4, so relief does bring the start forward there, and the new order gives that back.

**The banks (forecast: 0 within 10).** Wrong in the old order (62 us in e7 over e6, 92 in e4). For the change as a whole e5 and e6 take the same time, so order, banks and POOL's lighter load together come to 0; which makes up for the banks is not shown.

**The slower rival.** It gave 1518 by exposed round trips, near the measured time, but for a cause that isn't the one. Its sign did come: loads of sorted rows waited for the single writes, in the kernel after and in e14.

```profile
SPq L558 <- DMA rows<-GONE,ADR: 76.7, 8, 19.2
```

```profile
SPq L559 <- DMA rows<-GONE,ADR: 134.0, 10, 26.6
```

But SP's queue could bear that: taking e14's 134.0 us of waits away (e15) was worth 18 us, or nothing, of the rival's 192. That 1518 is near 1533 is luck.

**Span and median.** The 36.3 us between them don't lie around the span, as the first table has it. The execution profiled after took 1529.9 us for a span of 1528.0: 1.9. The rest is a difference between the execution traced before and the ones timed; it is in both times of the forecast and all but cancels in its 6.5%.

## What to carry to other kernels

Look at the shape of every new DMA before its bytes: a 4 KB write of 1024 single elements left this core's DMA at a median of 24 to 50 GB/s for the next 8 us and cost 3 to 4 us of kernel time, and the same bytes in 128 runs cost 0.5% for all 16. On an engine that works in order, price a new step as a hole for what is queued behind it, not as a share of the engine's idle time. And an engine's relief is worth only what waits for its load; what that is, a run tells that takes the work away and puts nothing in its place.

## What the runs showed of the hardware

- *Table write.* Adjacency packets of 2048 bytes, of which most take 84 to 93 ns, last up to 6.1 us behind 1024 packets of 4 bytes, though these themselves, at the write of 1013.38, have all started within 1.6 us of the issue. Indirect DMAs of 128 single elements from POOL showed nothing of the kind (e18, 0.995). What in the DMA makes the difference is not settled.
- *POOL beside DVE.* A small POOL instruction takes some 0.20 us while DVE is idle, as from 1061.3 to 1070.8 in e14 (DVE's 9.54 us above), and up to 1.5 us beside a pass of DVE: the `HUB` passes below, with two inputs, run beside the instruction at 1075.46, and the `OHB` pass, with one fp16 input, beside that of 1.10 us at 1074.28. L1552 of the kernel after, a cast of 128x2, has a minimum and median of 186 ns and a maximum of 1571. The Trainium skill, "GPSIMD Engine Reference", section "Key points", says that the engine shares its SBUF interfaces with VectorE, with contention for DVE instructions in a 2-port perf mode or with two SBUF inputs. The trace agrees on the two inputs, and the factor is up to 8; in which mode the `OHB` pass ran, it doesn't say.

```profile
1074.07 1.22 DVE L1227 TENSOR_SCALAR OHB<-POSB 128x4096 f16<-128x4096 f16 x1
1075.20 1.68 DVE L1309 TENSOR_TENSOR HUB<-HUB 128x1472 f32<-128x1472 f32 x1
1076.81 1.68 DVE L1310 TENSOR_TENSOR HUB<-HUB 128x1472 f32<-128x1472 f32 x1
```

```profile
L1552 POOL CAST ADR<-AT x16: 186/186/1571, 116.4 to 1331.7; 128x2 int32<-128x2 f32 x16
```

- *Sets of runs.* The kernel before took 1373.9 to 1444.6 us from set to set, 5%, and the two extremes came from one chip; expectations above that put this down to the chip say too much. The ratio of one and the same edited kernel went from 1.021 to 1.047.
- *Open.* Which of POOL's later steps, besides `COEF`, hands its arrears on; whether DVE's waits for PE are latency or clock; which of order, banks and POOL's lighter load pays for which; whether the held loads cost 18 us or nothing; and an order made for the measured prices, which was not tried.
